# ScalarE instead of VectorE makes the near group's two-tile one-hots in a graph-attention stage

## What is computed

```python
xc = x[row]; xn = x[col]
h = relu(xc @ W1[:d] + xn @ W1[d:] + b1)
mask = sigmoid(h @ W2 + b2)[:, 0]
seg_sum = segment_sum(mask, row)
w = mask / (seg_sum[row] + 1e-09)
agg = segment_sum(w[:, None] * xn, row)
```

## Time and profile before

| | us |
|---|---|
| median of three executions | 4378.5 |
| the profiled execution, whole | 4369.24 |
| its span in the profile | 4367.5 |
| span of the 136 steps' near copies, first to last | 2736.1 to 4271.9 |

### The profile page before, as it was taken

The page is one execution under the profiler, slowest core; times in us unless marked ns, Lnnn a source line. Parts: engine busy times, 40 slices in busy tenths (PEclk is TensorE's granted clock), DMA queues, the critical chain, the costliest instruction groups (busy, mean ns, idle before and its releaser), DMA issues. The chain is left out here.

```text
span 4367.5 us, 95747 instructions
## 1 busy us (share of the span) xinstructions
PE 3569.9 (82%) x20539; PEld 2439.5 (56%) x20540; DVE 3158.9 (72%) x12757; ACT 2150.9 (49%) x6722; POOL 1555.6 (36%) x1256
## 2 busy tenths in 40 slices
PE   4868882698888999986997996888888888888883
PEld 2367771333333444433444444777777778777783
DVE  8999987698888888873003005888888888888886
ACT  0078884266677888872003003444444444444444
POOL 0068874000000000001002002777777777777770
PEclk8855555799999999997998998999999999999996
DMA  2011113001111222224874882444444444444451
GB/s 47 1 10 15 15 17 81 10 34 51 68 68 77 95 93 103 94 86 187 303 276 165 304 297 85 144 137 141 138 138 142 136 141 138 137 138 140 141 134 40
DMA packets 276115, 498.31 MB, mean 114 GB/s; under 512 B 92068, under 2 KB 192571, under 8 KB 275883
## 3 DMA queue, kind: packets, MB, share of 16 engines
q1 hardware_dynamic: 209550, 347.01, 23.8%
q0 software_dynamic: 66336, 149.10, 12.4%
HBM read 391.18 MB, written 104.79 MB: 114 GB/s over the span
## 5 line engine op out<-in xcount | busy, mean ns | idle before, releaser
L1684 POOL DMA_INDIRECT xs<-edge_table,ea_row_stage x1088 | 1104.7, 1015 | 448.9 <-issue 432.7
L1868 PE MATMUL ea_psa<-xs,slot_dst 128*128 128x129 f32 x3264 | 458.5, 285 | 231.3 <-DVE agg_t L1782 231.2
L1868 PEld LDWEIGHTS ea_psa<-xs,slot_dst 128*128 128x128 f32 x3264 | 416.2, 195 | 264.3 <-DVE agg_t L1782 257.5
L1235 PE MATMUL a_agg_ps<-a_adj_ring,parts 128*128 128x512 f16 (+1 forms) x2548 | 523.6, 369 | 46.0 <-DMA a_adj_ring<-adjacency 45.9
L1902 ACT ACTIVATE slot_dst<-ea_onehot,ea_mask 128x128 f32<-128x128 f16 x1632 | 535.7, 399 | 13.2
L1782 DVE TENSOR_TENSOR agg_t<-agg_t,ea_psa 128x129 f32 x1632 | 460.5, 282 | 109.9 <-PE ea_psa L1868 97.5
L1034 PE MATMUL ab_agg_ps<-ab_adj_stage,parts 128*128 128x512 f16 x1911 | 529.6, 388 | 0.0
L1896 ACT ACTIVATE ea_mask<-ea_dot,b 128x4 f32<-128x4 f32 x408 | 121.3, 297 | 771.7 <-DVE slot_src L1807 771.7
L449 ACT ACTIVATE dst_step<-iota,dst_low_bias 128x128 f16<-128x128 f16 x1188 | 358.1, 401 | 216.0 <-PEq L474 213.0
L429 POOL DMA_INDIRECT records<-both_parts,record_row x98 | 348.5, 3556 | 314.8 <-ACT both_parts L455 291.8
L1375 POOL TENSOR_TENSOR parts<-xs,parts 128x896 f16<-128x896 f32 x7 | 13.2, 1881 | 1224.7 <-ACT parts L1369 1224.7
(11 more groups left out here) (379 smaller groups left out, 6463.6 us busy)
## 6 DMA issues: line engine op xcount, KB each, us to landing
a_adj_ring<-adjacency SPq DMA_DIRECT2D x182, 896.0 KB, 4.6
ea_low_rows<-low_rows SPq DMA_DIRECT2D x411, 128.0 KB
adjacency<-ab_adj_stage SPq DMA_DIRECT2D x91, 512.0 KB, 2.6
adjacency<-ab_adj_stage SPq DMA_DIRECT2D x91, 384.0 KB, 2.3
ea_near_rows<-near_rows SPq DMA_DIRECT2D x137, 128.0 KB
xs<-edge_table,ea_row_stage POOLq DMA_INDIRECT x1088
edge_table<-vx SPq DMA_DIRECT2D x12, 512.0 KB, 2.9
ea_row_stage<-row_columns SPq DMA_DIRECT2D x272, 2.0 KB
```

The costliest lines, as they stand in the source:

```text
L1235: ins = nc.tensor.matmul(ps[:, h, 0:width], lhs(r, t), ring[:, g % SLOTS, k * DB:k * DB + width], start=t == 0 and r == 0, stop=t == NT - ...
L1684: nc.gpsimd.indirect_dma_start(got[:, h, g, k, 0:ROW], None, m.table, bass.IndirectOffsetOnAxis(ap=row_s[:, h, g, k:k + 1], axis=0)).then_ ...
L1868: ins = nc.tensor.matmul(psa[:, home, k, 0:AW], hot_m[:, g, k, :], what, start=True, stop=True)
```

## The change

`hot_d` is no longer made by VectorE's two comparisons. ScalarE makes it at the end of its step, in a new function `window`: two ACTIVATEs with Abs take |rel - id| into a new tile `away` (float16), two with Relu take relu(1 - away), which is one where the distance is zero. It waits for the row numbers and for `lookups(2)` of the current step, which still reads `hot_d`. TensorE's `lookups(2)` gets a wait for the new semaphore, and SyncE one before it loads row numbers. `window` runs once before the loop.

```diff
+                    sp.wait_ge(s_hot_d, t)
...
+            nc.vector.tensor_scalar(minus[:, :], m.row_ids[:, :], -1.0, None, ALU.mult)
...
-                ins = nc.vector.tensor_scalar(flat(hot_t[:, g, :, :]), lo[:, h, g, :], m.row_ids[:, 0:1], None, ALU.is_equal)
-                if g == NEARBY:
-                    for a in (0, 1):
-                        ins = nc.vector.tensor_scalar(flat(hot_d[:, a, :, :]), rel[:, h, :], m.row_ids[:, a:a + 1], None, ALU.is_equal)
-                ins.then_inc(s_hot_t[g], 1)
+                nc.vector.tensor_scalar(flat(hot_t[:, g, :, :]), lo[:, h, g, :], m.row_ids[:, 0:1], None, ALU.is_equal).then_inc(s_hot_t[g], 1)
...
+                    pe.wait_ge(s_hot_d, t + 1)
...
+            def window(h, i, n, first=False):
+                act.wait_ge(s_low[h], i)
+                if not first:
+                    act.wait_ge(s_u[NEARBY], n)
+                for a in (0, 1):
+                    nc.scalar.activation(away[:, a, :], rel[:, h, :], ACT.Abs, bias=minus[:, a:a + 1]).then_inc(s_away, 1)
+                for a in (0, 1):
+                    act.wait_ge(s_away, 2 * n + (a + 1))
+                    ins = nc.scalar.activation(hot_d[:, a, :, :].rearrange("p k e -> p (k e)"), away[:, a, :], ACT.Relu, scale=-1.0, bias=m.ones[:, 0:1])
+                ins.then_inc(s_hot_d, 1)
...
                     ins.then_inc(s_hot_m[g], 1)
+                window(1 - h, i * 64 + (64 + 64 * h), t + 1)
             act.wait_ge(s_ones, 2)
+            window(0, 64, 0, first=True)
```

More of the change, by code:

```diff
@@ L1640, in edge_attention @@
             sem(n) for n in ("v", "ones", "rows", "near_x", "add", "seen", "seen_sp", "seen_dve", "seen_pe", "read", "read_pe"))
+        away, minus = sb("away", [P, 2, G * P], F16), sb("minus_ids", [P, 2], F32)
+        s_away, s_hot_d = sem("away"), sem("hot_d")
         s_table, s_kept = sem("table"), sem("kept")
```

## The result

The changed kernel took 4662.9 us (median of 4 runs, 4661.0 to 4665.4) beside 4377.4 of the kernel before: a ratio of 1.0651, interval 1.0633 to 1.067. The forecast was 4619 us, range 4500 to 4705. The profiled execution's span grew from 4367.5 to 4659.3 us.

The account below looks back on a forecast made before the run. A ring of VectorE, TensorE and ScalarE was taken to bound the kernel, VectorE longest. New step 11.74 + 1.39 = 13.13 us against 11.376, times 136, plus 1.7: +240 on 4378.5, so 4619 us, range 4500 to 4705.

Parts of the forecast that it names:

- The ring at the full clock: Near copy to near copy through scores, products, `window`, `lookups(2)` and `sums(2)`: 11.74 us a step, 0.36 above 11.376.
- The handover to TensorE: From the end of `window` on ScalarE to TensorE's `lookups(2)`: 0.05 us a step.
- part (1): Stretch of a step from the near copy to the first lookup of `lookups(2)`; 6.14 us by the forecast's terms.
- How often the clock falls: TensorE's clock falls after its idle of about 2.5 us: 5 steps in 6, adding 1.39 us a step.
- Part (2): Stretch of a step from the first lookup of `lookups(2)` to `sums(2)`: 4.45 us plus 1.39 for clock falls.
- The price of one fall: A clock fall meeting `lookups(2)` on TensorE lengthens it by 1.67 us.
- Rival B: Clock falls every step and ScalarE's pairs do not overlap: 13.76 us a step, 4705 us, or 4657 with overlap; chance 0.18.
- VectorE's gain is off the ring: The 0.80 us a step saved before VectorE's fourth add does not shorten the new ring.
- A: Rival: TensorE's clock falls no more than before, only the ring counts, 50 us more, 4430 us; chance 0.10.
- C: Rival: `window` is done before `lookups(2)` is due, only VectorE's 0.80 us counts, -109, 4270 us; chance 0.03.
- D: Rival: Abs and Sigmoid need different ScalarE tables, two reloads a step, 349 us on top, 4970 us; chance 0.03.
- What is covered: SyncE's wait for a `window` two steps back holds neither row loads nor gathers; ScalarE is at worst some tenths late.

Follow-up runs that it names:

- wide_fill: Changed kernel plus three wide unread matmuls (six passes) filling TensorE's gap before `lookups(2)`: 4698.5 us, against 4793.9 for the unaltered changed kernel on the same chip.
- both: Changed kernel with two unread comparisons given back to VectorE at their old place: 4777.3 us, against 4799.1 for the changed kernel on the same chip.
- early: Changed kernel with the Abs passes moved to the start of ScalarE's step and the Relu passes behind the near copy: 4753.5 us, ratio 1.0086 to the kernel before.
- one_row: Changed kernel with SyncE's row-number broadcasts cut to one partition, results mostly wrong: 4660.5 us beside 4370.6 of the kernel before, ratio 1.0659.
- fill10: Changed kernel plus ten unread 128x512 matmuls in TensorE's order before its wait for `hot_d`: 5139.8 us, ratio 1.0976 to the kernel before.
- changed_again: The changed kernel unaltered, run again in a later set on another chip: 4799.1 us beside 4683.6 of the kernel before, ratio 1.0244.
- changed_third: The changed kernel unaltered, run once more in another later set: 4793.9 us beside 4684.7 of the kernel before, one run.
- abs_first: Changed kernel with the two Abs passes moved to the start of ScalarE's next step, Relu left last: 4763.5 us, ratio 1.0108 to the kernel before.

## Why the prediction was right

The sign, the range and the mechanism held. By its own steps:

- **The ring at the full clock.** Predicted 11.74 us, seen 11.79 to 11.93 in the seven steps without a fall. An Abs and a Relu took 707 ns each where 0.70 was taken (707 is also the estimate by the figure of the Trainium skill, "ScalarE: Activation LUTs", section "What ACT_TABLE_LOAD costs"), the four together 3512.37 to 3514.91, 2.54 us against 2.55; near copy to `window` 3.53 against 3.54; `sums(2)` to the copy 1.15 against 1.15.
- **The handover to TensorE was mis-sized.** Taken as 0.05 us from the earlier trace rows; the last Relu ends at 3514.91 and the first lookup begins at 3515.16, so 0.25. The 0.10 for the first weight load was right as well: `wide_fill` shows 4.45 from start to start. So part (1) was 6.14 in the sum and is 6.32: 0.18 x 136 = 24 us. The row that I took it from is a `sums` behind an add; why the lookup's start takes longer was not tried.
- **How often the clock falls was mis-sized.** 5 steps in 6 were taken, it is 128 of 135, or 0.95. Part (2) was 4.45 + 1.39 = 5.84 and is 6.03: 0.19 x 136 = 26 us. The 5 in 6 was a guess between two values, and no single gap predicts it: in the whole trace of before, 40 of the 66 steps with a gap of 2.1 to 2.4 us before `sums(1)` had a fall, and 1 of the 23 with one of 1.7 to 1.8, while at 2.55 us in each step it is nearly every one. The price of one fall, 1.67, was right to the hundredth: 6.12 - 4.45. Rival B had its "every step" nearly right and its missing overlap wrong; its 4657 with the overlap is the nearest figure of all. The two terms make 50 of the 52 us that are missing: the profiled executions differ by 291.8 where 240 were forecast.
- **VectorE's gain is off the ring.** Right: `both` returns the work and costs nothing. The forecast named the wrong place for its idle, though: VectorE does not wait for the near copy at L1807 but one instruction earlier, for `sums(2)` at the first add of group 2 (485 us), which comes due at the same moment.
- **The rivals.** A (no further falls, 4430) fell with the clock of 0.88. C (faster) fell with 2.55 us of idle ended by L1897 in 134 steps; the experiments show that its condition was one of order, not of load. D fell: there is one table load in the stage, as before. The bare step of `early`, where C's condition is met, was to give 4285 us and has not been measured without the unexplained waits.
- **What is covered.** Right in its effect, wrong in its reason. SyncE runs so far ahead that the `window` of two steps back is just ending when it asks for it: SyncE's new wait (L1718) stands 399 us in all, some 3 us a step, and holds the row loads. No cost of it is seen: only two waits of an engine in the stage, 3.4 us in all, are put down to a transfer. The bytes of the row loads do not matter either (`one_row`).

```profile
SPq L1718 <- ACT xs L1897: 399.2, 130, 3.6
```

- **The busy times.** 375 us more on ScalarE were named and it is 345. Busy time counts an overlap once, and the prediction's own 2.55 x 136 is 347.

## What to carry to other kernels

Before moving work to the engine with the most room, find where in that engine's own order it will stand: four passes of 0.7 us made the step 2.13 us longer at the end of ScalarE's step, because the next step's matmuls wait for them there and the clock falls in that wait, while the same passes split over two idle places left `lookups(2)` with no wait at all. When the move gathers TensorE's idle into one longer gap, add the fall of the clock to the sum: here 1.67 us for each fall, more than the whole ring at the full clock had lengthened (11.92 us against a mean of 11.38 before, some falls included). And take the ratio of two kernels from one chip only, and look for waits without a releaser before reading it: 1.065 in the first set (and in the last, with `one_row`) was 1.024 in another.

## What the runs showed of the hardware that was not expected

- The same kernel before took 4371 to 4377 us in two sets and 4684 to 4714 on three other chips, each within 0.3% in itself. The kernels traced on those three chips have waits that no recorded instruction ends.
- On such a chip 20 more short passes and their weight loads a step, 2.4 us of work in a gap of 2.55, cost 340 us (`fill10` against `changed_again`). The same busy time in 6 wide passes and their weight loads saved 95 (`wide_fill` against `changed_third`, on another such chip).
- A fall of the clock can follow two shorter gaps as well: in `abs_first` one of 1.66 us before `sums(1)` and one of 1.33 before `lookups(2)`, with 1.16 us of work between them, and pairs of 1.06 us behind them. I had expected none with gaps that short.

```profile
3547.62 1.16 PE L1869 MATMUL ea_psa<-xs,slot_dst 128*128 128x129 f32 x8 [1.66 <-DVE agg_t L1782]
3550.12 1.22 PE L1852 MATMUL ea_psv<-vx,xs 128*128 x2 [1.33 <-issue]
...
3552.41 1.06 PE L1852 MATMUL ea_psv<-vx,xs 128*128 x2
```
